# Four graph-convolution layers: row gathers with segment scans, or products with a matrix of edge counts

## The reference

```python
deg = jnp.zeros((n,), x.dtype).at[dst].add(1.0) + 1.0
dinv = jax.lax.rsqrt(deg)
enorm = (dinv[src] * dinv[dst])[:, None]
self_norm = (dinv * dinv)[:, None]
h = x
for l in range(4):
    hw = h @ Ws[l]
    agg = jnp.zeros_like(hw).at[dst].add(enorm * hw[src])
    agg = agg + self_norm * hw + bs[l]
    mean = jnp.mean(agg)
    var = jnp.mean(jnp.square(agg - mean))
    h = jax.nn.relu(ln_w[l] * (agg - mean) * jax.lax.rsqrt(var + EPS) + ln_b[l])
```

## Time and profile before

| | us |
|---|---|
| median of 3 runs | 17245.03 |
| lowest, highest | 17237.85, 17247.39 |
| the profiled execution, own time | 17227.0 |
| its span, first to last instruction | 17225.2 |

### The profile page before, as it was taken

One profiled execution on the slowest core, in us unless ns is written; L12 is line 12 of the kernel. 1 busy time (PEld: TensorE's weight loads), 2 busy tenths in 40 slices (PEclk: granted clock), 3 DMA queues, 4 the chain that ended last, 5 costly groups with the idle time before them and its releaser, 6 DMA issues.

```text
span 17225.2 us, 174055 instructions
## 1 busy us (share of the span) xinstructions
PE 6109.6 (35%) x34308; PEld 4983.1 (29%) x34308; DVE 5920.6 (34%) x10911; ACT 2729.8 (16%) x7620; POOL 12411.8 (72%) x12537
## 2 busy tenths in 40 slices
PE   3333335888877322221222212222222222242111
PEld 2222224666655222221222212222122222221111
DVE  5555554666656411113111131111221111421112
ACT  1111113555555000000000000000000000010000
POOL 6777776777750677776777767777767777777777
PEclk5555556777789555555555555555555555555555
DMA  2232222333368233332333323333333333122222
GB/s 85 77 77 77 77 76 67 91 91 91 91 139 165 60 83 82 83 83 62 84 83 83 83 64 81 84 83 83 72 73 83 84 83 82 39 65 66 66 66 59
DMA packets 2658674, 1387.24 MB, mean 81 GB/s; under 512 B 1359387, under 2 KB 2345423, under 8 KB 2658372
## 3 DMA queue, kind: packets, MB, share of 16 engines
q1 hardware_dynamic: 2102084, 834.12, 19.1%
q0 software_dynamic: 400960, 442.25, 12.8%
q10 hardware_dynamic: 155584, 110.36, 2.0%
HBM read 778.55 MB, written 606.93 MB: 80 GB/s over the span
## 4 chain that ended last, share of the span: by engine, by line
POOL 65%; issue 24%; PE 3%; DMA 2%; DVE 2%; ACTq 1%; ACT 1%; POOLq 1%; SPq 0%; DVEq 0%
POOL G L541 55%; POOL records L571 7%; POOL AG L1787 2%; POOL AG L589 1%; DMA AG<-runs,endrow_dst 1%; DVE S L1554 1%; ACTq L1176 1%; POOL fill_rows L556 1%; DMA records<-RT,IDX 1%; POOLq L538 0%; PE PS L841 0%; PE PS L705 0%; ACTq L1183 0%; PE PS L908 0%; ACTq L1179 0%
## 5 line engine op out<-in xcount | busy, mean ns | idle before, releaser
L541 POOL DMA_INDIRECT G<-node_table,IDX x9984 | 9843.5, 986 | 3375.7 <-issue 3120.6
L1356 DVE TENSOR_TENSOR_SCAN S<-M,S,PS 128x512 f32<-128x512 bf16 x1242 | 1587.5, 1278 | 8297.7 <-PE PS L640 8294.1
L640 PE MATMUL PS<-ident,G 128*128 128x128 f32 x4160 | 1155.4, 433 | 7659.4 <-DMA G<-node_table,IDX 7659.4
L640 PEld LDWEIGHTS PS<-ident,G 128*128 128x128 f32 x4160 | 743.8, 217 | 8073.0 <-issue 8021.3
L971 ACT COPY R<-PS 128x512 f32<-128x512 f32 x1248 | 730.3, 585 | 10167.9 <-PE PS L649 10167.9
L571 POOL DMA_INDIRECT records<-RT,IDX x1664 | 1641.3, 986 | 529.8 <-issue 487.9
L649 PE MATMUL PS<-ident,S 128*128 128x128 f32 x4992 | 1333.8, 422 | 26.4 <-DVE S L1356 9.8
L649 PEld LDWEIGHTS PS<-ident,S 128*128 128x128 f32 x4992 | 1052.5, 227 | 70.3 <-DVE S L1356 50.5
L841 PE MATMUL PS<-R 98*128 98x128 f32 x3328 | 1008.3, 397 | 0.0
L1348 DVE TENSOR_TENSOR OH<-iota_b,AG 128x392 bf16<-128x392 bf16 (+1 forms) x1664 | 927.1, 618 | 0.0
L841 PEld LDWEIGHTS PS<-R 98*128 98x128 f32 x3328 | 724.7, 269 | 0.0
(11 more groups left out here) (241 smaller groups left out, 10105.8 us busy)
## 6 DMA issues: line engine op xcount, KB each, us to landing
runs<-R SPq DMA_DIRECT2D x1040, 256.0 KB
M<-same_dst SPq DMA_DIRECT2D x1248, 128.0 KB
G<-node_table,IDX POOLq DMA_INDIRECT x9984, 2.5
runs_e<-RT SPq DMA_DIRECT2D x208, 272.0 KB, 2.7
fill_rows<-Z ACTq DMA_DIRECT2D x104, 512.0 KB, 2.6
runs_l<-R SPq DMA_DIRECT2D x208, 256.0 KB
G<-fill_rows SPq DMA_DIRECT2D x208, 256.0 KB
G<-records SPq DMA_DIRECT2D x416, 128.0 KB
```

The lines of the kernel that those rows point to most:

```text
L541: pool.indirect_dma_start(G[:, i, q * D:(q + 1) * D], None, table, bass.IndirectOffsetOnAxis(ap=IDX[:, i, q:q + 1], axis=0)).then_inc(sem( ...
L640: t = pe.transpose(bank(i % 2)[:, k * P:(k + 1) * P], src[:, k * P:(k + 1) * P], ident[:, :])
L1356: return dve.tensor_tensor_scan(S[:, i % 2, :], mask, data, init, op0, op1)
```

## The change

- **Matrix.** A byte matrix `adj` in DRAM, 105 blocks of 128 rows (source node) by 12,544 columns (destination), holds how often each edge occurs. It is zeroed by 105 DMAs of ScalarE's queue during the first pass. Counts of 256 and more go to 7 extra blocks (`NV`) whose row stands for 256 times a source.
- **Filling it.** After the second step SP reads the (dst, src) pair of each record, in `src` order, by 8 DMAs with 8-byte elements. VectorE finds runs of equal pairs by a scan and makes a cell number and a byte for each edge (cell numbers out of bounds are skipped). POOL scatters 1664 columns of 128 single bytes with indirect DMAs: 416 behind the first end gathers, the other 1248 behind the second. The layers start when all have landed.
- **Third step.** Masks and `dst` in `src` order come from the same pairs, written at once; the 16-byte reads, the `src` rows on TensorE (line 894), ScalarE's copies of them and the mask stores per chunk go. Masks are now read by SP as in the other passes.
- **Attribute pass.** It is a stage of its own between block 1 and the layers, with two sets of buffers, while POOL scatters.
- **Layers.** Features are kept transposed. Each layer projects, scales by `dinv` and splits the rows in three bf16 parts (`TERMS`); writes the table only for 7 gathers of the extra rows. Then for 7 groups of 1792 destinations and 105 blocks of sources: SP loads 128 x 1792 bytes, ScalarE (3 of 5) or VectorE (2 of 5) converts them to bf16, TensorE multiplies with 3 parts x 2 column ranges (512, 384) x 2 halves, each half into its own 64 partitions of PSUM. `own` adds the node's own row by products with the identity. Mean and variance come from `bn_stats` per group.
- **Around.** POOL's 98 gathers of edge ends come ahead of the layers' 7. The node table's rows lie in another order, so tables are written in 256-byte rows and the last pass reads its indices as 4-byte elements. Counts and starts are transposed on TensorE instead of going through DRAM. Layer parameters are loaded once.

```diff
+    AB = NJ + NV
+    CELLS = AB * P * NP
+    NOWHERE = AB * P
+    NK = AB // NR
+    TW = TILES // 8
...
+        TERMS = [T[:, 0:NJ * D // 2].bitcast(BF16), T[:, NJ * D // 2:NJ * D].bitcast(BF16), RTf[:, 0:NJ * D // 2].bitcast(BF16)]
+        RAW = [AGB[:, i * QW // 2:(i + 1) * QW // 2].bitcast(U8) for i in range(NR)]
+        RING = [AGB[:, NR * QW // 2 + i * QW:NR * QW // 2 + (i + 1) * QW].bitcast(BF16) for i in range(NR - 1)]
+        RING.append(M[:, :, :].rearrange("p s e -> p (s e)")[:, 0:2 * QW])
...
+            by_part = rec.rearrange("(q t) r -> q t r", q=P)[:, :, C_DST:RW]
+            for t in range(0, TILES, TW):
+                sp.dma_start(PAIRS[:, t:t + TW, :], by_part[:, t:t + TW, :]).then_inc(sem("pairs_in"), 16)
+            sp.dma_start(PN[1:P, 0:1, :], by_part[0:P - 1, TILES - 1:TILES, :]).then_inc(sem("pairs_in"), 16)
...
+            def adj_in(u, g, r, i):
+                if i in BY_ACT:
+                    sp.wait_ge(sem("conv_a"), u * (NA * NK) + (r * NA + (i // 2 + 1)))
+                else:
+                    sp.wait_ge(sem("conv_d"), u * (ND * NK) + (r * ND + (i // 2 + 1)))
+                sp.sem_inc(sem("turns"), 1)
+                sp.dma_start(RAW[i], adj[bass.ds(r * (NR * P) + i * P, P), bass.ds(g * (2 * QW), 2 * QW)])\
+                  .then_inc(sem(f"ring_in{i}"), 16)
...
+            def adj_out(t0, t1):
+                for t in range(t0, t1):
+                    pool.indirect_dma_start(
+                        adj_cells, bass.IndirectOffsetOnAxis(ap=CELL[:, t:t + 1], axis=0),
+                        VAL[:, t:t + 1], None, bounds_check=CELLS - 1, oob_is_err=False).then_inc(sem("adj_full"), 16)
+            pool.wait_ge(sem("adj_zero"), 16 * AB)
+            pool.wait_ge(*dve_at("cells_ready"))
+            adj_out(0, TILES // 4)
             runs_done(2)
             ends(AG, runs64, endrow[1], NG)
-
-            with pool.Fori(0, LAYERS) as l:
-                gather_pass("fwd", N4 - NCH + l * NCH, "gath_b", (l + 1) * NIT, l * TP + 2 * TP)
-                runs_done(l + 3)
-
-                pool.wait_ge(sem("h_ready"), l + 1)
-                pool.sem_inc(sem("pool_turns"), 1)
-                ends_layer(pool, l, sem, AG, runs64, endrow[0], NG, GT)
-
-            pool.wait_ge(sem("e_out"), 16 * NCH)
+            adj_out(TILES // 4, TILES)
...
+            def products(stat, rhs, base, x, start, stop):
+                for t in range(3):
+                    for c, w in SPLIT:
+                        for h in range(2):
+                            m = pe.matmul(PS[h * D:(h + 1) * D, base + c:base + c + w], stat(t), rhs[:, h * QW + c:h * QW + c + w],
+                                          start=start and t == 0, stop=False, skip_group_check=True)
+                return m
...
+            def dense(u, x, first, l):
+                base = 2 * x * 512
+                pe.wait_ge(sem("group_used"), u + 1)
+                for K in range(AB):
+                    i, r = K % NR, K // NR
+                    if i in BY_ACT:
+                        pe.wait_ge(sem("conv_a"), u * (NA * NK) + (r * NA + NA + i // 2 + 1))
+                    else:
+                        pe.wait_ge(sem("conv_d"), u * (ND * NK) + (r * ND + ND + i // 2 + 1))
+                    if K < NJ:
+                        products(lambda t: TERMS[t][:, K * D:(K + 1) * D], RING[i], base, x, K == 0, False).then_inc(sem("ring_free"), 1)
+                        continue
+                    if first and K == NJ:
+                        pe.wait_ge(sem("virt_ready"), l + 1)
+                    products(lambda t: VT3[:, t, (K - NJ) * D:(K - NJ + 1) * D], RING[i], base, x, False, False).then_inc(sem("ring_free"), 1)
+            def own(g, x):
+                base = 2 * x * 512
+                for b in range(GT):
+                    for t in range(3):
+                        for h in range(2):
+                            j = (g * 2 + h) * GT + b
+                            m = pe.matmul(PS[h * D:(h + 1) * D, base + b * P:base + (b + 1) * P], TERMS[t][:, j * D:(j + 1) * D],
+                                          ident_b[:, :], start=False, stop=t == 2, skip_group_check=True)
+                m.then_inc(sem("group_done"), 1)
...
+                for g in range(NG2):
+                    pe.wait_ge(sem("zl_ready"), l * NG2 + (NG2 + g + 1))
+                    if g >= 2:
+                        pe.wait_ge(sem("tt_ready"), l * NG2 + g - 1)
+                    for b in range(GT):
+                        o = (4 + 2 * (g % 2)) * 512 + b * P
+                        t = pe.matmul(PS[:, o:o + P], ZL[g % 2][:, b * P:(b + 1) * P], wls[:, bass.ds(l * P, P)], start=True, stop=True)
+                    t.then_inc(sem("proj"), 1)
+                pe.wait_ge(sem("terms"), l * NG2 + NG2)
+                for g in range(NG2):
+                    dense(l * NG2 + g, g % 2, g == 0, l)
+                    own(g, g % 2)
...
+                to_bf16(l * NG2, 0)
+                act.wait_ge(sem("pcols_ready"), l + 1)
+                act.sem_inc(sem("turns"), 1)
+                for g in range(NG2 + 2):
+                    if g < NG2:
+                        hidden(g, None, (sem("proj"), l * NG2 + g - 1) if g >= 2 else None)
+                    if 1 <= g <= NG2:
+                        act.wait_ge(sem("tt_ready"), l * NG2 + g)
+                        act.copy(cols(TERMS[0], g - 1), TT[(g - 1) % 3]).then_inc(sem("hi"), 1)
+                    if g >= 2:
+                        act.wait_ge(sem("rest"), l * NG2 + g - 1)
+                        act.copy(cols(TERMS[1], g - 2), REST[g % 2]).then_inc(sem("mid"), 1)
...
+            def to_bf16(u, r):
+                for i in BY_DVE:
+                    dve.wait_ge(sem(f"ring_in{i}"), u * (16 * NK) + (r * 16 + 16))
+                    dve.sem_inc(sem("turns"), 1)
+                    dve.wait_ge(sem("ring_free"), u * AB + (r * NR + (i + 1)))
+                    dve.tensor_copy(RING[i], RAW[i]).then_inc(sem("conv_d"), 1)
...
+                        dve.tensor_tensor(halves(TT[g % 3]), PS[:, o:o + QW].rearrange("p (b h d) -> p b h d", b=GT, h=2),
+                                          bc(dinv[:, g * 2 * GT:(g + 1) * 2 * GT].rearrange("p (h b) -> p b h", h=2), [P, GT, 2, D]),
+                                          ALU.mult).then_inc(sem("tt_ready"), 1)
...
+                    dve.tensor_tensor(cols(FM, g), PS[:, o:o + QW], DINVB[x], ALU.mult).then_inc(sem("group_used"), 1)
+                    dve.wait_ge(sem("group_used"), l * NG2 + g + 3)
```

More of the change, by code:

```diff
@@ L381, in step @@
                         runs_out(dst, c - 4, i, c - 4 + r0)
-                    if attr is not None and i == 3:
-                        if lead != "first":
-                            attr_out(attr + (it - 1))
-                        if lead != "last":
-                            attr_in(attr + it)
                 for i in range(4):
@@ new lines, in attr_step, with cols @@
+            def attr_step(d, x):
+                attr_pen(d + 1, 1 - x)
+                attr_copy(d, x)
+            attr_step(0, 0)
+            attr_step(1, 1)
+            with act.Fori(1, NCH // 2 - 1) as u:
+                for x in range(2):
+                    attr_step(u * 2 + x, x)
+            attr_step(NCH - 2, 0)
+            attr_copy(NCH - 1, 1)
+            for x in range(2):
+                act.wait_ge(sem(f"e_out{x}"), 8 * NCH)
+            def cols(t, g):
+                return t[:, g * QW:(g + 1) * QW]
@@ L1202, in _ @@
+            act.wait_ge(sem("pcols_ready"), LAYERS + 1)
+            act.sem_inc(sem("turns"), 1)
+            for g in range(NG2):
+                hidden(g, None, (sem("xl"), g - 1) if g >= 2 else None)
             root(4)
@@ new lines, in _ @@
+            for k in range(NV):
+                t = dve.tensor_scalar(vrow[:, k:k + 1], pidx[:, 0:1], float(NP + k * P), None, ALU.add)
+            then(t)
+            then(dve.tensor_scalar(W1, goes_on, float(NOWHERE), None, ALU.mult))
+            then(dve.tensor_tensor(W1, W1, own_s, ALU.max))
+            for k in range(NV):
+                c = slice(k * VW, min((k + 1) * VW, TILES))
+                t = dve.tensor_scalar(W2[:, c], W1[:, c], -1.0, vrow[:, k:k + 1], ALU.mult, ALU.add)
+            then(t)
@@ new lines, in _, with cols, halves @@
+            for x in range(2):
+                dve.wait_ge(sem(f"e_out{x}"), 8 * NCH)
+            then(dve.memset(ncol[:, :], float(NJ * D)))
+            then(dve.memset(ncol[D:P, :], float(NJ * D - (NP - n_nodes))))
+            dve.sem_inc(sem("pcols_ready"), 1)
+            dve.sem_inc(sem("group_used"), 1)
+            dve.sem_inc(sem("group_used"), 1)
+            def cols(t, g):
+                return t[:, g * QW:(g + 1) * QW]
+            def halves(t):
+                return t.rearrange("p (h b d) -> p b h d", h=2, b=GT)
```

781 lines of the change are left out of this document (483 added, 298 removed).

## The result

The changed kernel takes 13,659.5 us (median of four runs, 13,642 to 13,680) where the kernel before took 17,243.3 beside it: ratio 0.792, 95% interval 0.791 to 0.794. In a second comparison on another occasion it was 0.790 (0.789 to 0.791). 13,720 was forecast. From one occasion to another the kernel before moved by 45 us (medians 17,227 to 17,272), and executions of the kernel after lay between 13,604 and 13,680, so medians of different occasions compare to some 50 us only; smaller effects are read from the traces, stretch by stretch.

The account below looks back on a forecast made before the run. The prediction took POOL's row of indirect DMAs to bound the kernel. Matrix full at 7522, layers 3728, first layer 50 and remaining 2400 gave 13,700, or 13,720 for whole-kernel runs; range 13,300 to 15,300.

Parts of the forecast that it names:

- What bounds the kernel before, and what goes: Whole kernel: POOL's indirect DMAs bound it; the layers' four gather passes, 9047 us, go; two passes, 2400 us mainly, stay.
- The zeroing at +4: First gather pass: zeroing the matrix is hidden by POOL's pace, +4 us for odd late index loads; uncovered 460.
- Pair read 190: After the record scatter: reading 212,992 pairs at 14.6 ns per packet over 16 engines takes 190 us, bounds 100 to 400.
- Scatter and third step: Cells to full matrix: 590 for 416 scatters beside the third step, 130 ends, 1604 for 1248 scatters, 40 normalisation: 2364 us.
- the rival of dear single-byte writes: Matrix scatter: byte writes cost more than POOL's 1.28 us; at 4 us 18,200; chance 6% slower than before, 3% between.
- The attribute pass covered with 500 us to spare: Between block 1 and the layers: 208 chunks at about 4.5 us each, allowed 7.5, fit beside POOL's scatters.
- The tile at 1.20: Dense layers: one tile of 128 x 1792 bytes takes 1.20 us, so 735 tiles take 882 us per layer.
- the raw buffer's round: Dense tile loads: conversion, handing over, issue and landing take 5.6 to 6.1 us over five buffers, 1.12 to 1.22 per tile.
- Ahead of and behind a layer's groups: Each layer: conversions 5 us, projection and splitting 29 ahead of the groups; scaling and statistics 8 behind.
- First layer +50: First layer: POOL's 98 end gathers delay the overflow-row gathers that ScalarE waits for after half of group 0: +50 us.
- Feed-bound tiles: Rival, dense tiles: landings under load take 5 to 8 us, a tile 1.5 to 2.1; at 1.6, 14,900 us; chance 18%.
- Halves one after another: Rival, dense tiles: the column halves do not overlap, a tile takes 2.3 us, +3234, 16,950 us; chance 8%.

Follow-up runs that it names:

- its own run: The changed kernel with all products of a tile written to PSUM partitions 0 to 63, save each group's first tile: 16,843 us in one execution.
- six and six: The changed kernel with all six products of a tile's first column half ahead of all six of the second: 13,633 us in one execution.
- twelve and twelve: The changed kernel with two tiles' products together, twelve of the first column half, then twelve of the second: 14,801 us in one execution.

## Why the prediction came out

- **What bounds the kernel before, and what goes:** right, and this is what makes the forecast: the four passes went whole, and what stayed did so within 3 us in the tail. That the sum came within 60 us is in part luck, since misses of both signs cancel.
- **The zeroing at +4:** wrong. The first record comes 58 to 101 us later (2820 to 2863 against 2762), of which some 7 lie ahead of the first gather, where +6 for parameter loads was told; the rest, 52 to 95 against the 2768 without the zeroing, is the zeroing's. The step that failed is "hidden by POOL's pace": I looked for late index loads, and bandwidth was indeed there (share 0.44), but POOL's own instructions bound the pass, and the mean gather is 3 to 5% longer beside the zeroing (1225 to 1251 against 1194 ns), since more of them start together with a run of VectorE and are held for 3.03 us. The prediction used that very hold for the scatters of the third step and not here. Moved away, the loss goes.
- **Second step at its old length:** 16 us shorter (2131 against 2147). With the zeroing that makes the +78 at the last record.
- **Pair read 190:** 140. The price per packet was right and was turned into time as if packets on an engine took turns; the share of 142% shows that they do not.
- **The dinv_n store at nothing:** +40, by omission. The changed program has the store and VectorE's wait for it; the prediction has no step for either.
- **Scatter and third step:** 2406 for 2364. The 416 beside the third step took until 5836 (615 for 590), the later ones 1666 for 1644. POOL set the pace, as told; the rival of dear single-byte writes has no ground. That rival leaned on the Trainium skill ("DMA: Bandwidth & Descriptors", Specifications), which says that transfers under 512 B are read, changed and written back. If that happens here, it shows as no more than the 3 ns worked out above.
- **The attribute pass covered with 500 us to spare:** 590, and 570 by the run with a quarter of the scatters. (The prediction's own numbers, 5950 + 208 x 4.5 = 6886 against 7522, would have given 636.)
- **The tile at 1.20:** TensorE sets it at 1.135. The mis-sized term is the raw buffer's round, forecast at 1.12 to 1.22 and measured at 1.08 where it binds: loads land in 2.9 us by the median where I took 3.2 to 3.7. 735 x 4 x 0.065 = 191 us, against 167 gained in the layers; the first layer took 7 to 11 more than told, and each layer's start some 4. By the rule of the Trainium skill ("DMA: Bandwidth & Descriptors", Anatomy of one DMA) the estimate was 2.5 us, a round of 4.9 and TensorE as the limit, 150 us under my sum. The section tells it of GpSimd's path, and these loads are SyncE's; the trace lands between (2.9), and has TensorE as the limit, so the rule was the better guide. I had set it aside because "the landings shown above lie a little over that rule"; that reading was wrong for the larger one, 448 KB in 2.5 us, where the rule gives an estimate of 3.1.
- **Ahead of and behind a layer's groups:** 42 us forecast (5, 29 and 8); from the start of a layer's last product to that of the next layer's first it is 41.6 (8572.2 to 8613.8).
- **First layer +50:** 57 to 61, by the mechanism named, save that it is ScalarE's own place in its program that waits: TensorE would need the rows only 48 tiles later.
- **Rivals.** Feed-bound tiles: out, feed allows 1.08. Halves one after another: out, and priced by its own run at 2.27 us per tile (forecast 2.3).

## What to carry to other kernels

An edit that runs beside an engine's instructions is free only if these keep their length: compare the mean duration of the bounding instruction, not only the DMA share, and if it has grown, look at the shortest, the median and the longest too. Here the median had not grown at all; a tenth of the instructions were held by another engine, whose start the edit had shifted. A DMA queue's share can exceed 100%, so packets times price per packet is an upper bound of the time. And each wait on the path that sets the end must be checked for every semaphore it names: here one of them was for a store that could have been made 2000 us earlier.

## What the chip showed that I had not expected

Products with a 64-wide stationary operand on different column halves run at the same time without standing side by side in the program, and even start out of program order, as long as at most four earlier ones of the other half are unfinished: 0 us lost with six and six, 0.4 us per tile with twelve and twelve. The Trainium skill ("TensorE: Matmul & The Clock Gate", Part 3, The mechanism) says that matmuls start and end in strict program order; the line at 8899.95 above shows a start against it, 0.25 us before that of 8900.20: M is used by the fifth tile alone, and the fourth tile's last product is ahead of it in the program. A POOL gather that starts with a run of VectorE operations with two SBUF sources takes 3.03 us in place of 0.94, and a transfer on a third engine's queue can bring the two together. A store of 12,544 single elements took 39.8 us, 38.2 when issued early in the second step. And 128 single-byte writes to random places cost the DMA engines some 3 ns each.
